# Split q/k/v products, four-strip attends and row-paired offsets in the feed-forward blocks of a macaron kernel

## The reference

```python
for l in range(2):                                # _layer
    h = shift_token(x)                            # half of the features one token later
    q, k, v = split(h @ wqkv[l])                  # 128 -> 3 x 512, 8 heads of 64
    q, k = rotary(l2norm(q) * qs, l2norm(k) * ks)
    s = 8 * q @ k.T, masked to i-64 <= j <= i     # windows of 64 with one look back
    x = x + (softmax(s) @ v) @ wo[l]
    h = layernorm(shift_token(x)) * lg + lb
    a, g = split(h @ w1[l] + b1[l])
    x = x + (a * gelu(g)) @ w2[l] + b2[l]
```

## Time and profile before

| | |
|---|---|
| median of 3 runs | 2709.12 us (2707.49 to 2718.69) |
| the profiled execution, own time | 2701.43 us |
| its span | 2699.6 us |
| PE busy / weight loads | 2413.8 us (89%) / 1718.1 us (64%) |
| DVE, ACT, POOL busy | 1732.0 (64%), 1523.2 (56%), 985.6 us (37%) |
| mean granted TensorE clock | 0.96 |
| chain that ended last | PE 78%, DVE 7%, DMA 5%, ACT 5% |

### The profile page before, as it was taken

How to read it: one execution, slowest core, us unless ns; L and a number is a source line. 1 busy time by engine, 2 the same in 40 slices (tenths; PEclk the granted TensorE clock), 3 DMA queues, 4 the chain that set the end, 5 groups by cost and what they waited for, 6 DMA issues and landing times.

```text
span 2699.6 us, 47599 instructions
## 1 busy us (share of the span) xinstructions
PE 2413.8 (89%) x19142; PEld 1718.1 (64%) x19142; DVE 1732.0 (64%) x2796; ACT 1523.2 (56%) x2382; POOL 985.6 (37%) x672
## 2 busy tenths in 40 slices
PE   2899999999999869999789999999999995678666
PEld 2567676767676656666456666767667663666366
DVE  3676766777777547777466767677777755443444
ACT  0566666666666516555556666666666653335432
POOL 4554444443534110000054545453444423320342
PEclk8899999999999969999989999999999997889989
DMA  7000000079996000000110000000000000120013
GB/s 141 1 1 1 1 2 1 1 89 124 121 127 67 1 1 1 2 1 2 40 33 1 1 1 1 1 1 1 1 1 1 1 1 27 50 64 1 24 51 97
DMA packets 185181, 73.31 MB, mean 27 GB/s; under 512 B 79434, under 2 KB 180980, under 8 KB 184836
## 3 DMA queue, kind: packets, MB, share of 16 engines
q1 hardware_dynamic: 176948, 56.68, 16.2%
q0 software_dynamic: 5568, 10.12, 1.2%
q10 hardware_dynamic: 2448, 3.48, 0.6%
HBM read 24.05 MB, written 46.18 MB: 26 GB/s over the span
## 4 chain that ended last, share of the span: by engine, by line
PE 78%; DVE 7%; DMA 5%; ACT 5%; issue 2%; POOL 1%; ACTq 1%; SPq 1%; DVEq 0%; POOLq 0%
PE psum L1358 11%; PE psum L1281 8%; PE psum L1387 7%; PE psum L1340 7%; PE psum L1369 4%; PE psum L1289 4%; PE psum L1398 4%; PE psum L1334 3%; PE psum L1303 3%; PE psum L1336 3%; PE psum L1259 2%; DMA y_tokens<-tile_y,tile_x 2%; PE psum L1267 2%; PE psum L1307 2%; PE psum L1497 2%
## 5 line engine op out<-in xcount | busy, mean ns | idle before, releaser
L461 POOL TENSOR_TENSOR work<-work,rot_tables 128x512 f32<-128x512 f32 x256 | 443.3, 1752 | 647.6 <-ACT work L546 647.6
L469 POOL TENSOR_TENSOR work<-work 128x1024 f32<-128x1024 f32 x128 | 301.8, 2357 | 13.0 <-DVE work L864 3.1
L1281 PE MATMUL psum<-ffn_w,y_all 128*128 128x512 f32 x512 | 248.6, 608 | 8.1 <-POOL y_all L476 5.3
L864 DVE TENSOR_TENSOR work<-work,rot_tables 128x1024 f32<-128x1024 f32 x128 | 175.1, 1368 | 108.6 <-ACT work L546 108.6
L1019 DVE TENSOR_REDUCE small<-psum 128x4 f32<-128x1024 f32 x128 | 156.6, 1224 | 92.7 <-PE psum L1507 92.6
L1340 PE MATMUL psum<-work 64*128 64x128 f32 (+1 forms) x2048 | 193.3, 318 | 0.0
L881 DVE TENSOR_TENSOR work<-work,small 128x1024 f32<-128x1024 f32 x128 | 160.7, 1258 | 48.9 <-ACT small L560 47.0
L1387 PE MATMUL psum<-centered,ffn_w 128*128 128x256 f32 x768 | 187.8, 395 | 3.2 <-DVE centered L923 2.9
L657 ACT ACTIVATE work<-psum 128x1024 f32<-128x1024 f32 x128 | 131.0, 1023 | 100.4 <-PE psum L1514 100.4
L1340 PEld LDWEIGHTS psum<-work 64*128 64x128 f32 x2048 | 143.1, 187 | 47.9 <-issue 47.9
L476 POOL TENSOR_TENSOR y_all<-centered,squared 64x256 f32<-64x256 f32 x64 | 49.7, 777 | 333.7 <-ACT squared L606 331.1
(11 more groups left out here) (274 smaller groups left out, 5651.7 us busy)
## 6 DMA issues: line engine op xcount, KB each, us to landing
h_area<-mean_weights SPq DMA_DIRECT2D x16, 2048.0 KB, 24.2
tile_x<-h_area SPq DMA_DIRECT2D x78, 64.5 KB, 1.8
work<-y_tokens SPq DMA_DIRECT2D x8, 512.0 KB, 6.1
stage<-in_consts ACTq DMA_DIRECT2D x1, 3009.0 KB, 12.6
work<-in_x SPq DMA_DIRECT2D x4, 512.0 KB, 28.4
expert_w<-in_ew SPq DMA_DIRECT2D x1, 2048.0 KB, 8.4
expert_w<-in_ew SPq DMA_DIRECT2D x8, 256.0 KB, 6.6
out<-work SPq DMA_DIRECT2D x8, 256.0 KB, 3.5
```

What stands on the lines that cost most here:

```text
L461: last = pool.tensor_tensor(b[:, :, :, o_], a[:, :, :, i_], tab[:, l, 1, t, :, o_].unsqueeze(2).to_broadcast([P, 2, HEADS, 32]), ALU.mult)
L469: pool.tensor_tensor(rC[:, t, :], rC[:, t, :], rB[:, t, :], ALU.add).then_inc(f_sum, 1)
L864: dve.tensor_tensor(g(rC[:, t, :]), g(rA[:, t, :]), tab[:, l, 0, t, :, :].unsqueeze(2).to_broadcast([P, 2, HEADS, DH]), ALU.mult)\
L1281: last = pe.matmul(PS[:, 1 + t + g, :], Y[:, s, ts_], fw[:, l, g * INNER:(g + 1) * INNER], start=True, stop=True)
```

## The change

In the feed-forward block:

- q, k and v are computed in three products of operands split into a high and a low part of type F32R. POOL splits the input of each item (`split_h`: a copy and a subtraction of 128 x 256, at the end of its iteration), DVE splits wqkv once at the start. `qk(i, t)` and `v_proj` count on one semaphore.
- `scores` writes the masks of all three groups first, then the products; its wait for the next item's copy_qk stands ahead of them.
- `m_split` writes each maximum to two places 64 rows apart, in a 128-column tile that is otherwise zero; `m_T` turns all 128 columns and `m_out` copies 128 partitions.
- `scores_T` writes the masks of two groups, then waits for the turned maxima, adds the offsets of even and odd heads from rows 0 to 63 and 64 to 127, directly followed by the transposed products. The third group is as before behind f_u.
- `attend` uses four column strips of 32 for four heads: one set of denominators for both halves of a head's 64 outputs, and the outputs in two rounds z. `recips` works on 256 columns, `o_norm` reads them twice; `wo` is loaded head by head in the matching order.
- `x_var` stands before both attends.
- SBUF is laid out anew; the expert weights take the place of the feed-forward weights and are loaded after the second pass, and DVE waits for them only before the first expert tile.

```diff
+                def split_h(i):
+                    l, s = layer_of(i)
+                    if l == 0:
+                        pool.wait_ge(f_y0, 2 * (f * SEQS + s + 1))
+                    else:
+                        pool.wait_ge(f_res2, i - SEQS + 1)
+                    free(pool, f_qk, 3 * (i - 1))
+                    pool.tensor_copy(hh[i % 2][:, :], Y[:, s, 0:T]).then_inc(f_h, 1)
+                    pool.wait_ge(f_h, 2 * i + 1)
+                    pool.tensor_tensor(hl[i % 2][:, :], Y[:, s, 0:T], hh[i % 2][:, :].bitcast(F32), ALU.subtract)\
+                        .then_inc(f_h, 1)
...
+                    if k + 1 < ITEMS:
+                        split_h(i + 1)
...
-                    link(act.activation(rec[:, a, :], PS[:, (3, 0)[a], :], ACT.Ln))
+                    link(act.activation(rec[:, a, :], PS[:, (3, 0)[a], 0:T], ACT.Ln))
...
+                link(split(qw_hi[:, l, :], qw_lo[:, l, :], raw_qkv[:, l, :]))
...
+                    twice = lambda a: a.unsqueeze(2).to_broadcast([P, TILES, 2, HEADS])
+                    mn = mneg[:, :, :].rearrange("p t (g r) -> p t g r", g=2)
+                    link(dve.tensor_copy(mn[:, :, :, 0:HEADS], twice(mx)))
...
-                dve.tensor_copy(mT[0:2 * HEADS, :], PS[0:2 * HEADS, 7, 0:T]).then_inc(f_mTs, 1)
+                dve.tensor_copy(mT[:, :], PS[:, 7, 0:T]).then_inc(f_mTs, 1)
...
+            def three(out, hi, lo, w_hi, w_lo):
+                pe.matmul(out, hi, w_hi, start=True, stop=False)
+                pe.matmul(out, hi, w_lo, start=False, stop=False)
+                return pe.matmul(out, lo, w_hi, start=False, stop=True)
...
-                        pe.wait_ge(*((f_y0, 2 * (f * SEQS + s + 1)) if l == 0 else (f_res2, i - SEQS + 1)))
+                        pe.wait_ge(f_h, 2 * i + 2)
...
-                        last = pe.matmul(PS[:, 1 + t + g, :], Y[:, s, ts_],
-                                         fw[:, l, g * INNER:(g + 1) * INNER], start=True, stop=True)
+                        last = three(PS[:, 1 + t + g, :], hh[i % 2][:, ts_], hl[i % 2][:, ts_], qw_hi[:, l, ws],
+                                     qw_lo[:, l, ws])
...
+                    pe.wait_ge(f_cp, min(2 * i + 3, 2 * ITEMS * (f + 1)))
+                    for bs, hs, w, _, _, m in groups:
...
-                        last = pe.matmul(PS[0:2 * HEADS, 7, t * P:(t + 1) * P], mneg[:, t, :], eyeb[:, :],
+                        last = pe.matmul(PS[:, 7, t * P:(t + 1) * P], mneg[:, t, :], eyeb[:, :],
...
+                    def products(bs, hs, w, j, i0, m):
+                        rows_ = lambda h: slice(64 * (h % 2), 64 * (h % 2) + 64)
+                        for h in hs:
+                            o = (h - hs[0]) // 2 * w
+                            pe.matmul(PS[:, bs[h % 2], o:o + w], sel[rows_(h), h, :], mT[rows_(h), i0:i0 + w],
+                                      start=False, stop=False, skip_group_check=True)
...
+                    bands(*groups[0])
+                    pe.wait_ge(f_vsb, min(i + 2, ITEMS * (f + 1)))
+                    bands(*groups[1])
+                    pe.wait_ge(f_mTs, i + 1)
+                    products(*groups[0])
+                    products(*groups[1])
+                    free(pe, f_u, i)
+                    bands(*groups[2])
+                    products(*groups[2])
...
+                    for lo, hi, j, src in blocks:
+                        for q in range(4):
+                            last = pe.matmul(PS[32 * q:32 * q + 32, (3, 0)[a], lo:hi], ones64[:, 0:32],
+                                             PT[:, 4 * a + q, src:src + hi - lo], start=j == 0, stop=j == 1,
+                                             skip_group_check=True)
+                    last.then_inc(f_den, 1)
+                    for z in range(2):
+                        for lo, hi, j, src in blocks:
+                            for q in range(4):
+                                d = (4 * a + q) * DH + 32 * z
+                                last = pe.matmul(PS[32 * q:32 * q + 32, (4, 2)[a], z * T + lo:z * T + hi],
+                                                 V[i % 2][:, j, d:d + 32], PT[:, 4 * a + q, src:src + hi - lo],
+                                                 start=z == 0 and j == 0, stop=j == 1, skip_group_check=True)
...
-                    if mid:
-                        attend(i - 1, 0)
                     if pre:
                         x_var(n)
                     if mid:
+                        attend(i - 1, 0)
                         attend(i - 1, 1)
```

More of the change, by code:

```diff
@@ L330, in build @@
         N_C = 5 + 12
+        N_W = 6 + HEADS
         N_SMALL = 26
@@ L1288, in v_proj @@
                     for t in range(TILES):
-                        last = pe.matmul(PS[:, 5 + t, :], Y[:, s, t * P:(t + 1) * P], fw[:, l, 2 * INNER:3 * INNER],
-                                         start=True, stop=True)
-                    last.then_inc(f_v, 1)
+                        ts_, ws = slice(t * P, (t + 1) * P), slice(2 * INNER, 3 * INNER)
+                        last = three(PS[:, 5 + t, :], hh[i % 2][:, ts_], hl[i % 2][:, ts_], qw_hi[:, l, ws],
+                                     qw_lo[:, l, ws])
+                    last.then_inc(f_qk, 1)
                 def scores(i):
@@ L1304, in scores @@
                                       start=True, stop=False, skip_group_check=True)
+                    for bs, hs, w, t, k0, _ in groups:
                         for h in hs:
@@ L1320, in scores_T @@
                 def scores_T(i):
[L1321 to L1324 removed]
+                    groups = (((2, 3), range(4), J0W, 0, 0, mst0), ((5, 6), range(8), J1W, 1, P, mst1),
+                              ((0, 1), range(4, 8), J0W, 0, 0, mst0))
@@ L1325, in scores_T, with bands @@
+                    def bands(bs, hs, w, j, i0, m):
                         q = len(hs) // 2
-                        if n == 0:
-                            pe.wait_ge(f_cp, min(2 * i + 4, 2 * ITEMS * (f + 1)))
-                        elif n == 1:
-                            pe.wait_ge(f_vsb, min(i + 2, ITEMS * (f + 1)))
-                        else:
-                            free(pe, f_u, i)
                         for b in bs:
-                            for u in range(q):
-                                pe.matmul(PS[:, b, u * w:(u + 1) * w], sel[:, hs[0] + 2 * u + bs.index(b), :], mT[:, i0:i0 + w],
-                                          start=u == 0, stop=False, skip_group_check=True)
@@ L1342, in scores_T @@
+                            last = pe.matmul(PS[:, bs[h % 2], o:o + w], kT[rows_(h), h // 2, j * P:(j + 1) * P],
+                                             qT[rows_(h), h // 2, i0:i0 + w], start=False, stop=True, skip_group_check=True)
                         last.then_inc(f_st, 1)
+                    pe.wait_ge(f_cp, min(2 * i + 4, 2 * ITEMS * (f + 1)))
+                    bands(*groups[0])
+                    pe.wait_ge(f_vsb, min(i + 2, ITEMS * (f + 1)))
+                    bands(*groups[1])
```

98 lines of the change are left out of this document (43 added, 55 removed).

## The result

The changed kernel takes 2596.91 us (median of 4 runs, 2589.86 to 2600.00) against 2709.16 of the kernel before on the same chip (4 runs, 2707.49 to 2718.69): ratio 0.9575, 95% interval 0.9545 to 0.9605. It is 112 us faster, where 127.5 were forecast (2580). The profiled execution took 2595.3 us, its span is 2593.4. PE is busy for 2249.1 us (87%), DVE 1717.4 (66%), ACT 1460.7 (56%), POOL 1089.9 (42%).

What follows compares the result with a forecast made beforehand. PE, without gaps, was taken as the bound, with a DVE/ACT chain next behind it. Iteration gains of 54 + 82 = 136 us less 8.5 of charges give 127.5 off 2709.1, rounded to 2580; range 2540 to 2640.

Steps and rivals of the forecast that it cites:

- Transposes to up: From qk_T's transposes to up: the ACT and DVE chain needs 9.8 us against 10.41 now, gain 0.61 an iteration.
- x_var: Moved ahead of both attends, it waits uncovered for resid2 after down: net +1.04 us in iterations that normalise a new sequence.
- scores_T: Offsets in two row groups: PE work -0.96 us to 4.33; third group waits 0.4 for gated in plain iterations.
- Attends: Two attends with four column strips take 3.4 us; gain 1.24 in iterations normalising a new sequence, 1.1 in plain ones.
- Hidden work: split_h on POOL comes 0.5 us late where a new sequence is normalised, absorbed by the first stretch's slack; expert weights cost nothing.
- up and x_mean: -0.1 (no change of shape before up): PE at up and x_mean: 0.1 us less an iteration, since no change of tile shape precedes up.
- Some 29: Of 32 pre iterations, those that also normalise a new sequence, some 29 run in the full pipeline, 1.87 us gained each.
- I take 0.22: Each split q/k/v product of 512 columns takes 0.22 us, three replace 0.86: PE work -1.27 an item (-0.84 at 0.24).
- Charges: Splitting wqkv on DVE 5.9 us, first split_h of each pass 2 x 1.3, expert weights no cost: total 8.5 us.
- PE as bound: Rival: PE stays the bound because other engines move up with it, so all 3.98 us an item counts: 2492; chance 0.05.
- Short strips that don't overlap: Rival: in the attends' 24 four-wide steps strips don't overlap, 3.2 us more an item: 2785 us; chance 0.05.
- New waits beyond those counted: Rival: further waits of 0.5 to 1.2 us an item, from POOL against DVE, late gated or split_h: 2630; chance 0.15.

Runs made afterwards that it cites:

- f32: The changed kernel with q, k, v as single f32 products again, no split_h and no split of the weights: 2575.54 us, ratio 0.9525.
- the offsets alone: The kernel before with only the new m_split, m_T, m_out and scores_T: 2642.66 us, ratio 0.9758.
- The parts alone: The kernel before with one part each: four-strip attends 2636.42 us, new scores_T with its offsets 2642.66, split q/k/v products 2677.58, x_var ahead of both attends 2732.33.
- the split products alone: The kernel before with only split, split_h and three split products for q, k, v: 2677.58 us, ratio 0.9882.
- both mends with f32: The changed kernel with x_var between the attends, q's bf16 copy on DVE, and single f32 products for q, k, v: 2560.80 us, ratio 0.9447.

## Why the prediction was right, and where its sizes were off

The forecast of 2580 (own range 2550 to 2605) stands against 2596.9, and 2582.4 on a second chip, where the kernel before takes 2704.4. Its mechanism was right at each place that it named; one wait came that it didn't name.

- **Transposes to up.** 9.8 was the floor worked out from DVE and ACT. In the pre iteration the transposes are issued by 393.75 + 1.80 = 395.55 and up starts at 405.35: 9.80. DVE has no gap from 398.64 to 404.88. In plain iterations the stretch is 9.87 where the transposes wait for o_norm 0, and 9.80 in the first four of each pass, where they don't. That this chain holds the stretch is shown twice: by shortening it (q's copy on DVE, plain -0.38) and by giving PE more to do (f32, iterations within 0.08).
- **x_var.** Down to x_var is 2.73 (2.64 forecast), with 1.17 of wait; the move alone costs 1.06 in pre iterations (1.04 forecast), and taking it out of the change returns 0.96.
- **scores_T** takes 4.35 (4.33 forecast). The wait for gated in plain iterations is 0.21 (0.4 forecast): gated ends 0.2 later after the transposes than forecast, and PE comes 0.4 later.
- **Attends.** 3.40, as forecast, with 0.57 for the first denominators and 1.09 for the outputs. Four strips of 192 and 128 columns run at their columns alone, as those of 256 did in the earlier trace rows, with weight loads that hide. The Trainium skill ("TensorE: Matmul & The Clock Gate", Part 3: Packing small matmuls) has loads overlap only across row groups, which would have made this the term that decides; the trace disagrees, with 1.66 and 1.74 for the two attends (392.01 - 390.35, 393.75 - 392.01).
- **Hidden work.** split_h is 0.15 late, and nothing follows from it: cosines start 398.64 - 395.55 = 3.09 after the transposes, as in the kernel before. The prediction had 0.5 late as absorbed whole; with x_var between the attends it is 0.27 late in the median, and 0.12 of that reaches up, so 0.5 would have cost something. The expert weights are read 40 us after their last issue.

What was too large is the gain, 136 in the iterations where 115.7 came. In three parts:

- **The size of an iteration.** Pre: 25.80 for 25.5. The parts of the 0.28: up 2.69 for 2.59, down to x_var 0.09, x_var itself 0.07, scores_T 0.02. Plain: 23.99 for 23.8 (23.82 by the forecast's stretches): 0.10 for the transposes, 0.07 to up, 0.10 in up, less 0.09 in scores_T. The 0.17 as far as up is the wait that the prediction lacks: it counted all of the attends' 1.1 as gained and didn't ask what DVE has to finish before the second group of transposes. The first four plain iterations of each pass, without the wait, take the 23.80 of the forecast. 26 x 0.28 + 34 x 0.2 is 14. The step that failed most is "up and x_mean: -0.1 (no change of shape before up)". up took 2.65 in the offsets alone, where it didn't wait, so the shape is worth 0.04, not 0.1; and it took 2.69 wherever y_normed held it: the wait puts back what the changed shape saves.
- **The count.** "Some 29" pre iterations at full gain: between first transposes there are 13 full ones in each pass, 26. 3 x 1.87 is 6.
- **The split products.** "I take 0.22" was wrong; the bound beside it, 0.24, was near (0.235), and even it left out 0.1 for the first product after another shape. PE's work fell by some 3.4 an item, not 3.98 (3.98 - 1.27 + 0.72). It cost nothing in the forecast's sum, because this stretch isn't PE's any more: the waits in it are smaller instead, by the same sum 9.8 - (10.41 - 0.72 - 0.4 - 0.25) = 0.76 as an estimate, where 1.3 stood.

Charges: the two splits of wqkv take 2 x (0.96 + 1.76) = 5.4 on DVE (5.9 forecast), the first transposes come 3.8 later in the changed kernel's first profile and 6.5 in its second (7 forecast); over all traces with the splits it is 3.6 to 8.1.

The rivals. PE as bound (2492) fell with the f32 run. Short strips that don't overlap (2785) fell with the attends at 3.40. New waits beyond those counted (2630) came only as the 0.17 before up in plain iterations, far under the 0.5 to 1.2 an item that it takes.

The parts alone bring -74, -68, -30 and +24, -148 in sum; together they brought -112 and -122. The medians make this difference too large. By the iterations, the parts' gains add up to 1.87 in a pre and 2.34 in a plain one, 128 us, where the change brought 1.59 and 2.19, 116. These 12 us are what the parts share: the wider m_T (0.19) and the split products (0.64) shorten the same stretch, whose floor lets 0.61 through, and the scores in one round, not timed alone, bring nothing more there.

## What to carry to other kernels

When a gapless engine is relieved, look for the next gapless chain in each stretch between two hand-overs and work out its length first: here it told 9.80 to the hundredth in pre iterations (9.87 came in most plain ones), while what PE saved beyond it was worth nothing. Then look at the end of the stretch that gets shorter, too: what the other engines have to finish before the next one can start comes nearer by as much. A step of 0.6 us that waits for the operation just ahead of it belongs behind work that covers the wait; moved ahead, it cost 0.96 to 1.06 an iteration and a fifth of the whole gain. And measure the parts both ways, alone on the old kernel and taken out of the new one: the split products gave 30 us alone and nothing inside, until the chain itself was shortened.

## What the runs showed of the hardware that was not expected

- Products of split operands with 512 columns start 0.23 to 0.24 us apart, not 0.22 as the columns alone were taken to give, and the first behind the transposes is followed only after 0.32. So three in place of one f32 matmul save 0.12 us (half of 1.72 - 1.48), not 0.21.
- The cast of the maxima on DVE has a median of 0.56 us over the passes for 128 x 32 elements in the changed kernel, and of 0.56 for 128 x 16 in the split products alone; it was 0.49 for 128 x 16 before and is 0.44 for 128 x 32 in both mends with f32. So twice the elements cost nothing that shows. In 62 of its 64 executions a GpSimd operation runs beside it; in the two without one it takes 0.17 to 0.18 in each of these four traces.
- The subtraction of split_h on GpSimd takes 1.60 to 1.71 us in each of the 32 executions of the changed kernel beside DVE's qk_norm (L902, two inputs in SBUF), and 0.64 to 0.73 in the other 32, of which 30 run beside DVE's copy from PSUM (L871) and two beside nothing longer than 0.05 us; the median of 1.16 lies between two groups. In the attention stage it takes 0.72 each time. A duration of GpSimd read in one stage doesn't hold for another: look at what DVE does at the same time.
